# Mixture-of-experts layer behind a recurrent layer: blocks of 512 rows in place of 256

## What is computed

```python
def _swiglu(u, w1, w2, w3):          # w1, w2: (H, D), w3: (D, H), H = 682, D = 256
    h = u @ w1.T ; v = u @ w2.T
    return (sigmoid(h) * h * v) @ w3.T
gate = x @ Wg.T + routing_bias       # 8 experts
_, top_idx = top_k(gate, 4)
weights = softmax over the 4 chosen
out = _swiglu(x, Ws1, Ws2, Ws3)
for e in range(8): out += weights[:, e] * _swiglu(x, W1[e], W2[e], W3[e])
x = layernorm(x + out)
```

## Time and profile before

| | us |
|---|---|
| median of 3 runs | 1043.04 |
| lowest, highest | 1040.37, 1047.05 |
| span of the profiled execution | 1022.6 |
| median less span | 20.4 |
| mean granted TensorE clock | 0.992 of 2.4 GHz |
| shared blocks 2 to 8, 125.05 to 208.67 | 83.62 |
| experts, 208.67 to 933.43 | 724.76 |
| shared blocks behind, 933.43 to 1015.77 | 82.34 |

### The profile page before, as it was taken

One profiled execution on the slowest core, in us unless ns is written; L12 is line 12 of the kernel. 1 busy time (PEld: TensorE's weight loads), 2 busy tenths in 40 slices (PEclk: granted clock), 3 DMA queues, 4 the chain that ended last, 5 costly groups with the idle time before them and its releaser, 6 DMA issues.

```text
span 1022.6 us, 27284 instructions
## 1 busy us (share of the span) xinstructions
PE 986.2 (96%) x8630; PEld 839.9 (82%) x8630; DVE 587.4 (57%) x1673; ACT 525.9 (51%) x1367; POOL 532.9 (52%) x505
## 2 busy tenths in 40 slices
PE   9997989999999999999999999999999999999986
PEld 4556878878888888888988888888888888888875
DVE  3998877754554545445454545454454554545786
ACT  3665634544555545454454545554454554554465
POOL 3564057668233376237170016076888871884871
PEclk9997999999999999999999999999999999999999
DMA  7956134353433332532424123218864772885783
GB/s 245 227 122 170 22 93 124 100 179 105 152 94 100 94 100 81 176 102 43 144 52 139 47 52 128 48 47 180 129 95 80 125 116 52 118 125 88 94 158 106
DMA packets 167892, 113.84 MB, mean 111 GB/s; under 512 B 113436, under 2 KB 160031, under 8 KB 166688
## 3 DMA queue, kind: packets, MB, share of 16 engines
q0 software_dynamic: 30480, 59.41, 27.5%
q1 hardware_dynamic: 114960, 32.07, 15.1%
q10 hardware_dynamic: 22400, 21.76, 6.2%
HBM read 47.09 MB, written 40.96 MB: 86 GB/s over the span
## 4 chain that ended last, share of the span: by engine, by line
PE 75%; DVE 10%; issue 4%; DMA 3%; ACT 3%; POOL 3%; SPq 0%; ACTq 0%; DVEq 0%; POOLq 0%
PE psA L1024 50%; PE psB L1051 19%; POOL y_sum L722 2%; PE psB L1054 2%; DVE g_lo L1452 2%; DVE psC L1442 2%; PE psA L975 1%; DVE g_hi L1452 1%; ACT sil L837 1%; PE psC L1006 1%; DMA row_weights_odd<-rows_by_place 1%; DMA y_sum<-rows_by_place,place 1%; DVE work L1239 1%; ACT y_sum L923 1%; DMA work<-x_tok 1%
## 5 line engine op out<-in xcount | busy, mean ns | idle before, releaser
L837 ACT ACTIVATE sil<-psA 128x256 f32<-128x256 f32 (+1 forms) x510 | 187.2, 373 | 276.9 <-PE psA L1024 231.9
L1442 DVE SCALAR_TENSOR_TENSOR g<-psA,sil 128x256 f32<-128x256 f32 (+1 forms) x178 | 73.5, 414 | 308.0 <-ACT sil L837 307.9
L722 POOL DMA_INDIRECT y_sum<-rows_by_place,place x128 | 199.1, 1556 | 86.1 <-DMA rows_by_place<-eb 37.4
L1024 PE MATMUL psA<-xb_odd,work 128*128 128x256 f16 x2112 | 235.9, 273 | 1.8 <-issue 1.6
L1024 PE MATMUL psA<-xb,work 128*128 128x256 f16 x2046 | 228.5, 273 | 3.4 <-issue 1.8
L1024 PEld LDWEIGHTS psA<-xb_odd,work 128*128 128x128 f16 x2112 | 206.0, 98 | 27.1 <-issue 3.4
L1024 PEld LDWEIGHTS psA<-xb,work 128*128 128x128 f16 x2046 | 199.4, 98 | 28.6 <-issue 5.6
L1051 PE MATMUL psB<-work,g_hi 128*128 128x256 f16 x1320 | 220.7, 273 | 1.2 <-DVE g_lo L1452 1.0
L1442 DVE SCALAR_TENSOR_TENSOR psC<-psA,sil 128x256 f32<-128x256 f32 (+1 forms) x332 | 140.1, 422 | 79.7 <-ACT sil L837 73.2
L1051 PE MATMUL psB<-work,g_lo 128*128 128x256 f16 x660 | 179.9, 273 | 0.0
L669 POOL DMA_INDIRECT rows_by_place<-y_rows,place x96 | 95.7, 997 | 136.9 <-DMA rows_by_place<-y_rows,place 120.1
(11 more groups left out here) (161 smaller groups left out, 873.8 us busy)
## 6 DMA issues: line engine op xcount, KB each, us to landing
stage<-wpack POOLq DMA_DIRECT2D x9, 2176.0 KB, 9.3
rows_by_place<-eb ACTq DMA_DIRECT2D x63, 256.0 KB
work<-half_beta SPq DMA_DIRECT2D x8, 512.0 KB, 4.9
work<-x_tok POOLq DMA_DIRECT2D x8, 512.0 KB, 5.9
work<-xT SPq DMA_DIRECT2D x7, 512.0 KB, 4.5
rows_by_place<-y_rows,place POOLq DMA_INDIRECT x128, 2.5
y_sum<-rows_by_place,place POOLq DMA_INDIRECT x128
out<-y_sum ACTq DMA_DIRECT2D x4, 512.0 KB, 4.3
```

Of the source, the lines that this page charges most:

```text
L722: pool.indirect_dma_start(out=y_sum[:, n, :], out_offset=None, in_=xs, in_offset=bass.IndirectOffsetOnAxis(ap=place[:, k, n:n + 1], axis=0 ...
L837: act.activation(sil[r0:r0 + n, c % SLOTS, 0:T], psA[0:n, c % HVS, 0:T], ACT.Silu, scale=1.0 / (XS * WS)).then_inc(silu_ready, 1)
L1024: last = pe.matmul(dst, W[:, ws, k, ci, :], xb[slot][:, KD * xs_ + k, 0:T], start=(k == 0 and n == 0), stop=(k == KD - 1 and n == 2))
L1442: dve.scalar_tensor_tensor(gated_rows(g, c, 0, n, T), src, 1.0 / (XS * WS), sil[r0:r0 + n, c % SLOTS, 0:T], ALU.mult, ALU.mult).then_inc(g ...
```

## The change

Blocks have TF = 512 rows (JF = 4 groups) where there are as many. The shared part has 6 blocks ahead (256, 256, 512, 512, 512, 256 rows) and 4 behind (512, 512, 512, 256). An expert's remainder of row groups becomes a block of 128, 256 or 384 rows; a remainder of one behind a full block becomes 384 and 256 in place of 512 and 128. Blocks wider than 256 rows put each of a chunk's two results into a bank of its own, so `psA` holds two chunks; `down` puts two groups of rows into one bank of `psB`, in two turns (groups 0 and 2, then 1 and 3), since a bank's sums are started one after the other. `eb` now lies in the room of the first weights, some `xb` in `work`. VectorE's side work is given to the chunks of fewer and longer blocks, ScalarE normalizes a lot in one piece behind a block.

```diff
-    OWN = [[], [0, 1], [2], [3], [4], [5], [6]]
-    EXTRA = [0, 2, 2, 3, 2, 0, 0]
+    AHEAD_TILES = [JB, JB, JF, JF, JF, JB]
+    BEHIND_TILES = [JF, JF, JF, JB]
+    LOTS = [[9, 10, 0, 1, 2, 3], [11, 12, 4, 5, 6, 7], [13, 14, 8], [15]]
...
+        def up_out(c, side, r, end, T):
+            if T > TB:
+                return psA[r:end, 2 * (c % 2) + side, 0:T]
+            return psA[r:end, c % HVS, side * TB:side * TB + T]
+        def down_out(j, T):
+            if T > TB:
+                return psB[:, j // 2, j % 2 * D:(j % 2 + 1) * D]
+            return psB[:, j, 0:D]
...
             with eng.If(full > 0):
                 with eng.Fori(0, turns) as i:
-                    run(TB, first + 2 * i, rows_from(2 * i), 2 * w)
+                    run(TF, first + 2 * i, rows_from(2 * JF * i), 2 * w)
...
-            with eng.If(half > 0):
-                run(P, eng.snap(first + full), None if group is None else eng.snap(group + JB * full), 4 + w)
+            with eng.If(big > 0):
+                run(3 * P, after, rows, 4 + w)
+            with eng.If(rest > 1):
+                run(TB, last, last_rows, 6 + w)
+            with eng.If(rest == 1):
+                run(P, last, last_rows, 6 + w)
...
-            for i in range(S2):
-                lot = LOTS.index(i - 2) if i - 2 in LOTS else None
-                ffn_block(r + S1 + i, beside=None if lot is None else lambda c: norm_groups(lot, c, NC - 1))
-                if lot is not None:
-                    store(lot)
+            for i in range(NL):
+                ffn_block(r + NA + i, BEHIND_TILES[i] * P)
+                if i > 0:
+                    norm_groups(i - 1)
+                    store(i - 1)
...
+                room = 2 if T > TB else HVS
                 for c in chunks:
-                    before = c - 4 if c >= 4 else (c + 4 if c + 4 < NC else c) - NC
-                    pe.wait_ge(gated_ready, NC * g + before + 1 + HVS)
-                    last = side(psA[:, c % HVS, 0:T], 2 * c)
+                    if c == 0:
+                        pe.wait_ge(gated_ready, NC * g + HVS)
+                    elif c >= room:
+                        pe.wait_ge(gated_ready, NC * g + c - room + 1 + HVS)
+                    last = side(up_out(c, 0, 0, P, T), 2 * c)
...
-                for c in range(NC):
-                    pe.wait_ge(gated_low_ready, NC * g + c + 1 + SLOTS)
+                sides = [range(T // P)] if T <= TB else [range(0, T // P, 2), range(1, T // P, 2)]
+                for turn, js in enumerate(sides):
+                    for c in range(NC):
+                        if turn == 0:
+                            pe.wait_ge(gated_low_ready, NC * g + c + 1 + SLOTS)
...
-            ffn_block(2, beside=weigh, rows_at={3: (4, 0), 4: (4, 1)})
...
+            shared(2, {0: weigh, 1: rows((4, 0)), 2: rows((4, 1)), 3: rows((6, 0)), 4: rows((6, 1)), 5: rows((1, 0)),
+                       NC: rows((1, 1), (3, 0))})
+            shared(3, {1: rows((3, 1)), 2: rows((5, 0)), 3: rows((5, 1)), 4: rows((7, 0)), 5: rows((7, 1)),
+                       NC: sizes_and_first})
+            shared(4, {1: lows(2), 3: lows(3), NC: lows(4, 5)})
+            shared(5)
...
+            beside = [None,
+                      {1: first_of_lot(1, 0, LOTS[0][0:2]), 2: stats_of(0, LOTS[0][2:4]), 3: stats_of(0, LOTS[0][4:6]),
+                       NC: roots_of(0)},
```

More of the change, by code:

```diff
@@ L406, in build @@
-        for i in range(S2):
-            ORDER += [q for q in dict.fromkeys([S1 + i] + FINISH[i]) if q not in ORDER]
-        assert sorted(ORDER) == list(range(NS))
+                    run(TF, first + 2 * i, rows_from(2 * JF * i), 2 * w)
+                    more = eng.snap(full - 2 * i)
+                    with eng.If(more > 1):
+                        run(TF, first + (2 * i + 1), rows_from(JF * (2 * i + 1)), 2 * w + 1)
+            big = eng.snap((left + 1) >> 2, min_val=0, max_val=1)
+            rest = eng.snap(left - 3 * big, min_val=0, max_val=2)
@@ L1490, in _, with shared, sum_shared, rows @@
             t = early
-            def beside_first():
-                chosen_early()
-            ffn_block(0, beside=beside_first)
+            def shared(g, beside=None):
+                ffn_block(g, AHEAD_TILES[g] * P, beside)
+            def sum_shared(g):
+                add_shared(g, AHEAD_AT[g], AHEAD_TILES[g])
+            def rows(*steps_halves):
+                def run():
+                    for s, h in steps_halves:
+                        low_half(s, h)
+                return run
+            def lows(*which):
+                def run():
+                    for i in which:
+                        first_low(i)
+                return run
+            def sizes_and_first():
+                pads()
+                sizes()
+                first_low(0)
+                first_low(1)
+            shared(0, {1: chosen_early})
             logits(NSTEP - 1)
@@ L1535, in moments, with lot_moments @@
                 t.add(ins)
+            def lot_moments(lot):
                 t.wait()
[L1537 to L1544 removed]
+                for j in range(JB * len(LOTS[lot])):
+                    ins = dve.bn_aggr(nmv[lot % 2][:, j, :], stat[:, j, :])
+                if lot >= POOL_LOT:
+                    ins.then_inc(pool_moments_ready, 1)
+                else:
+                    t.add(ins)
@@ L1545, in inverse @@
+            def inverse(lot):
+                m = JB * len(LOTS[lot])
                 nmv_, nv_, nr_, na_, nb_ = (n[lot % 2] for n in (nmv, nv, nr, na, nb))
```

455 lines of the change are left out of this document (241 added, 214 removed).

## The result

The kernel after takes 1115.44 us (median of 4 runs, 1112.60 to 1117.19), the kernel before 1041.70 us (4 runs, 1035.91 to 1047.05): ratio 1.069, 95% interval 1.063 to 1.076. It is 7% slower; the forecast was 1047 with a range to 1064. The profiled run of after took 1112.6 us for a span of 1110.9.

The account below looks back on a forecast made before the run. TensorE, busy for 96% of the span, was taken as the bound: matmul count times spacing, plus holes. Terms -3.9 ahead, +3.8 experts, +2.4 behind, +1.5 clock gave a span of 1026.4; with 20.4 kept, 1047 us, range 1028 to 1064.

Parts of the forecast that it names:

- How many blocks there will be: Experts: 27 blocks of 512 rows, 6 of 384 and 3 of 256, 36 in place of 69.
- the matmul time: TensorE: 216 ns per 512-column matmul; a 512 block takes 14.26 + 6.99 = 21.25 us, two old ones 21.40.
- The hole at the end of a 512 block: In down, TensorE waits for VectorE's low part of chunk 5: 0.5 us, 27 times; none at 384 rows.
- The rival of shorter ends: The chain at a block's end is shorter or starts earlier, and starts are in time: 1024.5 us; chance 0.19.
- The hole at the start: Chunk 2 waits for chunk 0's product: 0 us (to 0.5) in 512 blocks, 1.0 us in six 384 blocks.
- Late ScalarE: ScalarE's way around a block's edge exceeds 3.6 us, so each wide block waits 0.4 more: 1062 us; chance 0.16.
- With more code variants I put 7.4 (5 to 11): Experts' stage: gaps at loop ends and expert changes, 5.7 us before, become 7.4 us.
- Behind the experts: Shared blocks behind: 84.8 us, +2.4, with waits before chunk 2 of 3.3 us and, before the last block, 2.6.
- The clock: TensorE's clock may fall in long holes: 1.5 us added (0 to 10); as a rival +15, 1062 us, chance 0.08.
- Before the experts, 79.7: Shared blocks ahead, from 125.05: 79.7 us in place of 83.62, -3.9, with holes of 5.2 us in place of 8.7.
- the median of the runs is 20.4 above the span; I keep that: Whole kernel: the median of 1043.04 lies 20.4 us above the profiled span, and this is added unchanged.
- The spacing rule: Skill's rule: a 512-column matmul every 131 ns, a 512 block 15.6 us, in all 862 us; chance 0.01.

Follow-up runs that it names:

- a_short_loop: Kernel after with TensorE's loop over expert pairs shortened from 2,400 to 1,790 instructions, its unused 128-row form left out: 1074.9 us, ratio 1.021.
- b_never_run_600: Kernel before with 600 matmuls that never run added inside TensorE's loop over expert pairs: 1114.3 us, ratio 1.067.
- _150: Kernel before with 150 matmuls that never run added inside TensorE's loop over expert pairs: 1049.6 us, ratio 1.006.
- theory A: Not a run but the experiments' explanation: TensorE's loop over pairs of experts has grown past what it keeps loaded, so instructions are brought again each turn.
- b_tail_600: Kernel before with 600 matmuls that never run placed behind TensorE's loop over expert pairs, jumped over once: 1053.3 us, ratio 1.003.
- a_ahead_256: Kernel after with the nine shared blocks ahead of the experts in 256 rows each, side work as before: 1090.8 us, ratio 1.043.
- a_both_shifted: Kernel after with 256-row shared blocks ahead, loop shortened to 1,790 instructions, and 54 matmuls that never run ahead of the loop: 1066.3 us, ratio 1.016.
- a_short_threes: Kernel after with the shortened loop, first scatter issued three at a time with all landing before the next, second in pairs: 1050.6 us, ratio 1.002.
- b_threes: Kernel before with the first scatter issued three at a time, all landing before the next three, second in pairs: 1037.4 us, ratio 0.989.
- 9: Kernel before with one scatter in flight in place of three (first) and two (second): 1068.8 us, ratio 1.020.
- 10: Five kernels, variants of before and after, with scatters issued in pairs or threes that all land before the next go out: medians 1037.4 to 1060.0 us.
- 7: Kernel after with GpSimd's first scatter held back until the shared blocks ahead of the experts are added: 1143.4 us (one run).
- 8: Kernel before with all 128 indirect scatters made plain transfers of the same bytes to places known beforehand: 1029.5 us, ratio 0.980.

## Why the prediction was wrong

The forecast missed by 68 us. By stage, in the profiled run: 4.8 us before 125.05 (129.83), 18.6 ahead, 41.3 in the experts, 0.6 behind; 1047 and these make 1112.3, against 1112.6 measured. (Ahead: 117.0 against 79.7 and the 18.7 us of "median above span" that the forecast carried along, 20.4 less the 1.7 that lie around the span of after.)

- **How many blocks there will be, and the matmul time: right.** 36 blocks; 215.8 ns measured for 216; 14.24 and 7.54 us for 14.26 and 6.99 with 0.5.
- **The hole at the end of a 512 block: right.** The row marks 0.38 us, from the chain named, and none in a 384 block; by the starts down takes 0.55 more than the 6.99 (7.54), for the forecast 0.5. The rival of shorter ends did not come: the block takes 21.79 us for 21.75.
- **The hole at the start: right in the kernel after.** None before chunk 2 of a 512 block behind another; 0.93 for 1.0 in three of the six 384 blocks, 0.32, 0.48 and 0.57 in the others. Late ScalarE, the rival, did not come there; at changes of expert, where the unforeseen holes stand, this kernel can't show it (below).
- **"With more code variants I put 7.4 (5 to 11)" failed.** This is the term of the sum that decided. 27 x 21.79 + 6 x 16.9 + 3 x 10.7 = 721.8, so the gaps and slow stretches in the experts are 48 us. I had counted the variants as branches to be walked over, 1.7 us more in all, and not as instructions that have to be held. The trace of before could have raised the question: q8 moves no packet from 480 to 940 us in it, while the loop turns two more times, so the loop was held, and it was about to double. The price is what the pairs of runs show: 35.5 us (after against `a_short_loop`), 53.8 (`b_never_run_600` against `_150`).
- **What is left of the same term with the loop held** is 12.6 us (734.4 - 721.8), still over 7.4. Half of it stands at five changes of expert: the up of an expert's first 512 block takes 15.1 to 16.2 us there in place of 14.25, some 6 us in all. In the one shown ScalarE's first silu starts 4.9 us after the up (381.79 against 376.92); between blocks of one expert it starts after 3.2, and the forecast had 3.6. So "I take 0" for the start of a 512 block failed at changes of expert, in the way of the rival of late ScalarE. In the kernel after, the holes of theory A stand in these places. ScalarE and TensorE in `a_short_loop`, expert 0 to 1:

```profile
381.79 1.18 ACT L857 ACTIVATE sil<-psA 128x512 f32<-128x512 f32 x2 [3.39 <-issue]
...
383.24 7.08 PE L1039 MATMUL psA<-xb,work 128*128 128x512 f16 x32 [0.98 <-DVE g L1498]
```

- **Behind the experts: right.** 3.24 for 3.3 and 2.59 for 2.6 before chunk 2 of the last two blocks, both for VectorE's product:

```profile
1069.02 12.05 PE L1039 MATMUL psA<-xb,wshared 128*128 128x512 f16 x42 [3.24 <-DVE g L1499]
...
1096.44 2.14 PE L1039 MATMUL psA<-xb,wshared 128*128 128x256 f16 x18 [2.59 <-DVE g L1499]
```

The clock cost 3.0 there (20.46 - 14.25 - 3.24; mean granted clock 0.76 of 2.4 GHz over the 12.1 us behind the hole) for the 1.5. In return the ends of the blocks before, forecast at 1.1 and 0.9, were the plain 0.55, so that the total is closer than its terms.
- **Before the experts, 79.7: right as a count, wrong as a time.** With the starvation taken away the stage takes 80.5 us. What failed is the step "the median of the runs is 20.4 above the span; I keep that". A profiled run 20 us shorter than the median was the trace's way to say that it had missed something that the other runs have. `b_never_run_150` and `b_tail_600` have the same instructions ahead of the experts as the kernel before, and that stage takes 98.7 and 105.9 us in them, not the 83.62 of the earlier trace rows: 15 and 22 more, on both sides of the 18.7 that the forecast carried. No run of the kernel before on record is under 1035.9 us, and the profiled one, by the 1.8 us that lie outside the span in other runs, would be at some 1024.4, an estimate. So both kernels are starved, and the trace of before was by luck free of it. The kernel after is starved for some 18.6 us more than that. How much of it is the wide blocks' and how much chance stays open: under starvation blocks of 256 rows took 101.4, 107.0 and 102.0 us in variants of the kernel after, wide ones 117.0 and 123.7. `a_ahead_256` against after (1090.8 to 1115.4) and `a_both_shifted` against `a_short_loop` (1066.3 to 1074.9) speak for the wide blocks being hit harder; by which step was not tried.
- The 4.8 us before 125.05 vary by run: the same code got there at 124.7 to 131.5 us in variants of the kernel before. They can't be laid to the change.
- **The spacing rule** of the Trainium skill (the last rival) was wrong here: 215.8 ns, not 131.

Without both losses the change still costs more than was forecast. `a_short_threes` has 1050.6 us and a ratio of 1.002 (0.998 to 1.006), but to a kernel before that is itself starved, and its nearness to 1047 is luck: the starvation that the forecast carried is gone from it, and 15.6 us more in the experts and 7.4 more ahead stand in its place. Like for like it is `a_short_threes` against `b_threes`, taken together: 1050.6 to 1037.4, 1.3% slower, where the forecast had 3.8 us or 0.4%; in pairs, 1055.6 to 1043.1, it is 12.5 us. By stage the threes differ by 3.8 us less ahead without the waits (82.2 and 86.0) for the forecast 3.9 less, by 9.8 more in the experts for 3.8, of it 2.0 in the wait shown above, and by 3.3 more behind for 3.9. So ahead and behind the count was right, and in the experts it was some 4 to 6 us short even with the loop held.

## What to carry to other kernels

Before adding forms of a block to a loop, count the instructions of the loop per engine and look at the packets of the instruction queues while it turns: none means that it is held. TensorE here held 1,545 and not 2,400, and 1,790 only where the loop began at some places. If the profiled run is far from the median, find out what the others have before using its stages. Beside indirect transfers from GpSimd in a long unbroken row the other engines were starved in most profiled runs; a pause after two or three took this away, and was worth it only where the rows were not urgent. And when a loss is taken out of the kernel after, take it out of the kernel before too, or the comparison flatters the change.

## What the runs showed of the hardware that I had not expected

- A loop of TensorE of 2,400 or 2,445 instructions was brought anew in each turn: 53 to 55 packets of 16 KB in place of 21, and holes of 5.5 to 14.4 us where it turned, for which the profile has no releaser. In the 15 us around the first hole five packets came, and the mean granted clock was 0.78 of 2.4 GHz. The Trainium skill (Runtime: NRT & Kernel Launch, Instruction fetch mechanics) says that TensorE's instruction memory has 128 KiB, 2,048 instructions, filled in blocks of 16 KiB, 256 instructions, and that a taken branch to a place outside the two loaded pages has to wait for the fetch. The trace agrees in the 16 KB and in the waits. It does not agree with two pages, 512 instructions: from 480 to 940 us, over two turns and more, the loop of 1,240 moved no packet and that of 1,545 one. By the figure of 2,048, 1,790 instructions fit, and they did in two of three places.
- 111 instructions that never run, ahead of the loop, won 24 us (1090.5 to 1066.3).
- Starvation by indirect transfers of GpSimd that follow at some 1.3 us: TensorE then starts matmuls in steps that are multiples of some 0.71 us (155.04, 156.44, 158.57, 160.71 above), and VectorE and ScalarE go on 10 and 14 us after what they wait for is recorded. Why is not shown. What is shown is that it went away with pauses between the transfers (9, 10), with no transfers beside the blocks (7), and with plain ones, which had pauses too (8); whether it needs the indirect form stays open.
